# One loop over the edge tiles, with a running maximum, where three loops stood

## The reference

```python
# third layer, last part: agg holds summed edge messages of each node
os1 = ssp(s_in @ w_f2o1_s / sqrt(2F));  os2 = os1 @ w_f2o2_s / sqrt(B)
ov2 = (v_in x w_f2o1_v / sqrt(2F)) x w_f2o2_v / sqrt(B)      # 3 components
x3  = layernorm(x2 + concat([os2, ov2]))

# fourth layer: attention over the edges that leave a node, 8 heads of 64
q, k, v = split(x3 @ W);  q = q * 64 ** -0.5
aw    = einsum('ehf,ehf->eh', q[src], k[dest])
m     = segment_max(aw, src)
e     = exp(aw - m[src])
denom = segment_sum(e, src)
out   = segment_sum(e / denom[src] * v[dest], src)
x4    = layernorm(x3 + out)
```

## Time and profile before

| | us |
|---|---|
| median of the runs shown (3 runs, 2404.39 to 2411.34) | 2409.9 |
| the profiled execution, its time | 2407.1 |
| its span, first to last instruction | 2405.4 |
| PE busy in the span | 1907.2 |
| DVE busy in the span | 1583.2 |
| ACT busy in the span | 1038.4 |
| POOL busy in the span | 1007.9 |

### The profile page before, as it was taken

The page is one execution under the profiler, slowest core; times in us unless marked ns, Lnnn a source line. Parts: engine busy times, 40 slices in busy tenths (PEclk is TensorE's granted clock), DMA queues, the critical chain, the costliest instruction groups (busy, mean ns, idle before and its releaser), DMA issues. The chain is left out here.

```text
span 2405.4 us, 24073 instructions
## 1 busy us (share of the span) xinstructions
PE 1907.2 (79%) x5516; PEld 938.7 (39%) x5516; DVE 1583.2 (66%) x2672; ACT 1038.4 (43%) x1968; POOL 1007.9 (42%) x1095
## 2 busy tenths in 40 slices
PE   5999995999999999999999790055487699967800
PEld 2444442444444444444444340033255444423300
DVE  5464552577777777777776060799568679867854
ACT  2353442455555555555554230244278623313332
POOL 2211112466665666666656532456322012224334
PEclk9999998999999999999999895555568799979855
DMA  7632113444444444444443633433333222227743
GB/s 259 244 130 58 18 22 56 164 158 151 153 158 144 159 155 146 163 147 156 157 142 136 199 64 48 114 84 88 101 126 123 104 90 106 106 79 193 211 136 110
DMA packets 159454, 310.19 MB, mean 129 GB/s; under 512 B 31890, under 2 KB 45107, under 8 KB 159127
## 3 DMA queue, kind: packets, MB, share of 16 engines
q1 hardware_dynamic: 126278, 233.65, 28.0%
q0 software_dynamic: 29760, 71.21, 13.1%
q10 hardware_dynamic: 3344, 4.51, 0.6%
HBM read 169.54 MB, written 139.76 MB: 129 GB/s over the span
## 5 line engine op out<-in xcount | busy, mean ns | idle before, releaser
L659 PE MATMUL d_p_h<-w3a,d_xT 128*128 128x512 f32 x640 | 290.5, 597 | 25.4 <-DMA d_xT<-in_xT 25.4
L659 PE MATMUL d_p_o<-d_w,d_uT 128*128 128x512 f32 x640 | 289.9, 596 | 3.0 <-ACT d_uT L734 3.0
L659 PE MATMUL d_p_p<-d_wr,d_x1T 128*128 128x512 f32 x640 | 289.0, 595 | 0.0
L550 POOL TENSOR_SCALAR d_small<-d_mv 128x1 f32<-128x1 f32 x160 | 81.9, 512 | 303.5 <-DVE d_mv L785 153.7
L816 DVE TENSOR_TENSOR d_zz<-d_yg,d_xbeta 128x512 f32<-128x512 f32 x80 | 138.5, 1731 | 98.9 <-POOL d_yg L867 98.9
L659 PEld LDWEIGHTS d_p_h<-w3a,d_xT 128*128 128x128 f32 x640 | 122.8, 192 | 180.4 <-issue 180.4
L659 PEld LDWEIGHTS d_p_o<-d_w,d_uT 128*128 128x128 f32 x640 | 122.1, 191 | 156.6 <-issue 152.0
L727 ACT ACTIVATE d_yn<-d_y,d_small 128x512 f32<-128x512 f32 x80 | 65.1, 813 | 230.6 <-POOL d_small L555 230.6
L659 PEld LDWEIGHTS d_p_p<-d_wr,d_x1T 128*128 128x128 f32 x640 | 116.1, 191 | 115.9 <-issue 115.9
L282 PE MATMUL m_p_H<-m_xT,m_w 128*128 128x512 f32 x320 | 147.3, 615 | 4.8 <-ACT m_xT L323 4.8
L755 ACT ACTIVATE d_x<-d_zz,d_small 128x512 f32<-128x512 f32 x80 | 65.1, 814 | 178.4 <-POOL d_small L555 178.4
(11 more groups left out here) (252 smaller groups left out, 4239.2 us busy)
## 6 DMA issues: line engine op xcount, KB each, us to landing
sum<-d_zeros SPq DMA_DIRECT2D x80, 260.0 KB, 2.1
sum<-m_tile_sum SPq DMA_DIRECT2D x10, 2048.0 KB, 7.8
d_xT<-in_xT SPq DMA_DIRECT2D x80, 256.0 KB, 2.7
d_z<-sum SPq DMA_DIRECT2D x80, 256.0 KB, 2.9
d_x<-in_x SPq DMA_DIRECT2D x80, 256.0 KB, 3.4
x<-d_x SPq DMA_DIRECT2D x80, 256.0 KB, 2.0
p<-d_p SPq DMA_DIRECT2D x80, 256.0 KB, 2.0
pair_p<-p SPq DMA_DIRECT2D x40, 512.0 KB, 3.8
```

The source lines that it names most:

```text
L550: nc.gpsimd.tensor_scalar(tmp, var, factor, add, ALU.mult, ALU.add).then_inc(done, 1)
L659: last = nc.tensor.matmul(out[:, :], lhsT[:, c, :], w[:, c, :], start=(c == 0), stop=(c == KB - 1))
```

## The change

The three loops become one (`values_phase`, names `f_`), of 25 steps. In step i tile `a = i` has its message sums gathered and its first product, `b = i-1` its second product and x3 rows, `c = i-2` its queries and keys, `d = i-3` its scores, maximum, weights and values, `e = i-4` is merged into the state. The state of a node is one row in a table of 528 floats: 8 heads of 64 sums and one denominator, and 8 maxima. A tile gathers its nodes' rows, takes the larger of the old maximum and its own, weighs its values with reference to that new maximum, scales the old sums by exp(old - new), adds its own sums and writes the rows back; the next tile's gather waits for that write. The two tables of sums and maxima, the gather of final maxima and the accumulating scatter go.

Further parts: the scores are spread by a store to a DRAM row and a load broadcast to 128 partitions, on SP, in place of the diagonal and the product with ones; x2 is added on PE through the identity, the vector part of the second product is written to PSUM with a step of 3, its factor is put into the weights once, and ACT copies the result to `y`; the softplus is done per tile; `p_O`, `p_R`, `p_k` and the tile for queries and values are single; two reciprocals stand in `o_` for one; two table fills per node tile stand for three. The pairs follow a written plan: 3, 2, 2, then 1, 2, 1, 2, ... per step.

```diff
+def plain_plan(steps):
+    plan = [3, 2, 2] + [1 + i % 2 for i in range(steps - 3)]
-                sp.dma_start(rows(k.sum3, i), zeros[:, :]).then_inc(tables_set, 16)
-                sp.dma_start(rows(k.max3, i), lowest[:, :]).then_inc(tables_set, 16)
+                sp.dma_start(rows(k.state, i), empty[:, :]).then_inc(tables_set, 16)
...
         @block.sync
+            for step in range(STEPS):
+                t = step - 3
+                if 0 <= t < T:
+                    sp.wait_ge(aw_done, t + 1)
+                    sp.dma_start(k.aw_rows[t, :].rearrange("(p h) -> p h", h=HEADS), k.scores[:, t, :]
+                                 ).then_inc(aw_out, 16)
+                    sp.wait_ge(aw_out, 16 * (t + 1))
+                    if t:
+                        sp.wait_ge(cand_done, t)
+                    sp.dma_start(spread[:, :, :].rearrange("p e h -> p (e h)"),
+                                 k.aw_rows[t:t + 1, :].to_broadcast([P, P * HEADS])).then_inc(spread_in, 16)
+                for _ in range(HERE[step - 1] if step else 0):
+                    if pair + 2 < PAIRS:
+                        pair_load(nc, k, sp, pair + 2)
+                    pair_store(nc, k, sp, pair)
+                    pair += 1
...
         @block.gpsimd
+            def gather_sums(u):
+                if u >= AHEAD:
+                    n = turn_number((u - AHEAD) // 2, 2 + u % 2)
+                    pool.wait_ge(turned, n + 1)
...
+            def gather_state(t):
+                if t:
+                    pool.wait_ge(gone, 16 * t)
...
+            def scatter_state(t):
+                pool.wait_ge(merged, t + 1)
...
+            for step in range(STEPS):
+                for u in (2 * step + AHEAD, 2 * step + AHEAD + 1):
+                    if u < 2 * T:
+                        gather_sums(u)
+                t = step - 4
+                if 0 <= t < T:
+                    scatter_state(t)
+                    if t + 1 < T:
+                        gather_state(t + 1)
...
         @block.tensor
+            def second(t, s):
...
+                if u:
+                    pe.wait_ge(y_done, u)
...
+                nc.tensor.matmul(p_R[:, :], k.ident[:, :], rows_of(t, s), start=True, stop=False)
+                vector = p_R[:, B:D].rearrange("p (d c) -> p c d", c=3)
+                for c in range(4):
+                    last = nc.tensor.matmul(p_R[:, 0:B] if c == 0 else vector[:, c - 1, :],
+                                            outT[t % 2][:, s, c * P:(c + 1) * P],
+                                            (w2s if c == 0 else w2v)[:, :], start=False, stop=(c == 3))
...
+            for step in range(STEPS):
+                second(b, 0); turn_x3(c, 0); turn_x3(c, 1); second(b, 1); turn_sums(a, 0)
+                queries(c); first(a, 0); turn_sums(a, 1); values(d); first(a, 1); keys(c); tile_sums(d)
...
         @block.scalar
+            for step in range(STEPS):
+                second_product_out(b, 0); x3_turned_out(c, 0); x3_turned_out(c, 1)
+                second_product_out(b, 1); sums_turned_out(a, 0); away_from(d); query_out(c)
+                first_product_out(a, 0); sums_turned_out(a, 1); x3_rows(b); first_product_out(a, 1)
+                weights(d); state_factors(d); logarithms(a)
+                for _ in range(HERE[step]):
+                    pair_normalise(nc, k, act, pair)
+                    pair += 1
...
         @block.vector
+            def new_maximum(t):
+                buf, top = old[t % 2], new[:, ATT:STATE]
+                dve.wait_ge(old_in, 16 * (t + 1))
...
+                nc.vector.tensor_tensor(top, buf[:, ATT:STATE], buf[:, STATE:STATE + HEADS], ALU.max
+                                        ).then_inc(new_top, 1)
...
+                nc.vector.tensor_tensor(less[:, :], k.scores[:, t, :], top, ALU.subtract).then_inc(less_done, 1)
+                nc.vector.tensor_tensor(fall[:, :], buf[:, ATT:STATE], top, ALU.subtract).then_inc(fall_done, 1)
...
+            for step in range(STEPS):
+                scores(d); merge(e); moments(b, 0); moments(b, 1); pair_leaky(pair)
+                if extra == 1: pair_moments(pair)
+                tile_maximum(d)
+                if extra > 1: pair_moments(pair)
+                new_maximum(d); weigh_values(d); scale_state(d); softplus(a)
+                for _ in range(extra - 1): pair_leaky(pair); pair_moments(pair)
```

More of the change, by code:

```diff
@@ L52 @@
 PAIRS = NODE_TILES // 2
-PAIRS_Q, PAIRS_S, PAIRS_V = 10, 14, 16
+STATE = ATT + HEADS
 LOG2 = 0.6931471805599453
@@ L1107, in reciprocal_deviation @@
     act.wait_ge(done, base + 2 + n)
-def spread_over(steps, n):
-    return [(i * n) // steps != ((i + 1) * n) // steps for i in range(steps)]
+def plain_plan(steps):
+    plan = [3, 2, 2] + [1 + i % 2 for i in range(steps - 3)]
+    assert sum(plan) == PAIRS
+    return plan
 def pair_load(nc, k, sp, j):
@@ new lines, in values_phase @@
+        cand = k.filters[:, :, :, :].rearrange("p t c f -> p (t c f)")[:, KB * 2 * D:KB * 2 * D + HEADS * P].rearrange(
+            "p (h e) -> p h e", h=HEADS)
+        away = sb("away", [P, P])
+        less, both = sb("less", [P, HEADS]), sb("both", [P, HEADS, HD + 1])
+        old = [sb(f"old{i}", [P, STATE + HEADS]) for i in range(2)]
+        new = sb("new", [P, STATE])
+        fall, factor = sb("fall", [P, HEADS]), sb("factor", [P, HEADS])
+        p_T = [ps(f"p_T{i}", [P, D]) for i in range(2)]
@@ L1424, in _ @@
         def _(pe):
-            pe.wait_ge(w_in, 64)
[L1427 to L1462, removed]
+            def turn_sums(t, s):
+                u, n = 2 * t + s, turn_number(t, 2 + s)
+                pe.wait_ge(sums_in[u % AHEAD], 16 * (u // AHEAD + 1))
+                if n >= 2:
+                    pe.wait_ge(turned_out, n - 1)
+                for c in range(4):
+                    last = nc.tensor.transpose(p_T[n % 2][0:2 * F, c * P:(c + 1) * P],
+                                               sums[u % AHEAD][:, c * 2 * F:(c + 1) * 2 * F], k.ident[:, :])
+                last.then_inc(turned, 1)
@@ new lines, in product, with queries @@
+            def product(out, xT, w, done):
+                for c in range(KB):
+                    last = nc.tensor.matmul(out[:, :], xT[:, c, :], w[:, c, :], start=(c == 0), stop=(c == KB - 1))
+                last.then_inc(done, 1)
+            def queries(t):
+                pe.wait_ge(turned_out, turn_number(t + 2, 0) + 1)
+                if t:
+                    pe.wait_ge(vw_done, t - 1)
+                    pe.wait_ge(q_out, t)
+                product(p_qv, srcT, k.wqk[:, :, 0:D], q_done)
@@ L1824, in _ @@
+                if 0 <= d < T:
+                    tile_maximum(d)
+                if extra > 1:
+                    pair_moments(nc, k, dve, pair)
+                    pair += 1
+                if 0 <= d < T:
+                    new_maximum(d)
+                    weigh_values(d)
+                    scale_state(d)
+                if a < T:
+                    softplus(a)
+                for _ in range(extra - 1):
                     pair_leaky(nc, k, dve, pair)
@@ L1897, in _ @@
                 b, c = g % 2, g % BUFS
+                heads = [sums[c][:, s, 0:ATT].rearrange("p (h f) -> p h f", h=HEADS) for s in range(2)]
                 dve.wait_ge(sums_in[c], 32 * (g // BUFS + 1))
```

643 lines of the change are left out of this document (290 added, 353 removed).

## The result

The changed kernel takes 2452.99 us (median of 4 runs, 2449.69 to 2454.42) where the kernel before took 2407.14 us on the same chip (4 runs, 2402.78 to 2411.34). The ratio is 1.0191, with a 95% interval of 1.0170 to 1.0213. The forecast was 2454 us. The profiled execution took 2452.36 us against 2407.08 us, so 45.3 us more where +44 had been worked out.

A forecast was written before the change was run, and what follows sets the result against it. A chain across engines, not any engine's work, was taken as the bound. Summed steps ended the rows at 2352 against 2304.0, 48 us more, less up to 5: +44, giving 2451, plus 2.8 for the median: 2454 us, range 2385 to 2510.

The forecast's parts named there:

- The chain of a long step: From softplus to softplus after two pairs, through ACT, PE, POOL and the state's landing and gather: 29.2 us before clock and landings.
- The second path: Beside the chain in long steps: scores' store, broadcast, pair's load at 15.7 us, then pair, maximum and subtractions ending at 25.4.
- POOL's wait: POOL's gather for turned sums stands ahead of the state's scatter, to 18.9 us; removing it wins little in long steps.
- The long step: A step after two pairs: 29 to 37 us, taken as 32; the clock up to 4, landings 3.4 more at worst.
- The start: DVE's first pair at 1733.9 us as before, step 0's softplus at 1742, step 1 29 us; fewer table fills and starts save up to 5.
- The gap from the last rows to the o stage: The 9 us from the last rows' end at 2304.0 to the o stage's start at 2313 were to stay.
- The drain: Five last steps, set by DVE's list: together 87 us, plus 2.6 for the last normalisation, ending at 2352.
- DVE's work: DVE's busy work in the merged loop: 9.0 us a tile and 6.66 a pair, 446 us, 11 below before.
- The costs put at nothing: The maximum's read with step 8, at most double 1.22 us, hidden; the second product's write with step 3, up to 17 us.
- (a): Rival: the work sets the pace, 17 full steps average 23.5 us, 2389 us; gain below 24.7 us a step; chance 0.20.
- (b): Rival: idle stretches keep PE at 1.2 GHz, long steps 38 and short 30 us, 2550 us; chance 0.06.
- (c): Rival: the added chains cancel exactly what two drains give back, 2410 us; chance 0.04.

The follow-up runs named there:

- the six products: Changed kernel with six unread products on PE where it waits for ACT's copy in the long steps: 2452.89 us, ratio 1.0216 to the kernel before.
- The first experiment: Changed kernel with POOL's list alone reordered, the state's scatter and gather ahead of the two gathers of message sums: 2408.41 us, ratio 1.0020.
- POOL's and ACT's order mended: Changed kernel with state ahead of gathers on POOL and the second pair's normalisation moved to the next step on ACT: 2412.71 us, ratio 1.0032.
- the lists mended: Changed kernel with POOL's state first, ACT's second normalisation later and SP's pair loads ahead of the scores' store and broadcast: 2374.13 us, ratio 0.9865.
- ACT's 7 alone: Changed kernel with ACT's list alone changed, a step's second pair normalised in the next step ahead of the x3 rows: 2443.26 us, ratio 1.0160.
- SP's a loss of 12 alone: Changed kernel with SP's list alone changed, pair loads issued ahead of the scores' store and broadcast: 2460.19 us, ratio 1.0239.
- PE doing ten products for nobody: Changed kernel with POOL's and ACT's lists reordered, plus ten unread products before the tile sums of long steps: 2401.52 us, ratio 0.9982.

## Why the prediction held

**The chain of a long step was right link by link.** Counted from the end of the softplus at 2072.12: PE's wait for ACT ends at 9.9 us (forecast 9.9). POOL's gather is issued at 19.4 (17.5 and up to 4 for the clock; 17.7 with the clock kept by the six products), and the scatter at 21.1 (18.9 and the same). The state's row is there at 28.2 (25.8 with nothing for the clock, so up to 29.8 with it), and the softplus ends at 30.9. The second path has its pair's load at 16.2 (15.7) and its maximum and subtractions done at about 26 (25.4). POOL's wait, ACT's turn and DVE's wait for `f_old` stand in the list of waits as named, and PE's granted clock is 0.82 (near 0.8).

**POOL's order was the cause of the loss.** The first experiment moves only it, and 1.0191 becomes 1.0020. "Taking POOL's wait away would thus win little in these steps" is right too: 1.7 us a long step. The gain is in the short steps, 4.8 us each.

**The sum, term by term.** The middle column is the forecast.

| | forecast | measured |
|---|---|---|
| softplus of step 0 ends | 1742 | 1744.5 |
| steps 1 to 3 | 82.5 | 86.2 |
| steps 4 to 16: seven short | 168 | 166.0 |
| six long | 192 | 184.2 |
| steps 17 to 19 | 76.5 | 76.7 |
| draining and last normalisation | 89.6 | 96.1 |
| the end of the rows (2352 in the forecast, rounded up on the way) | 2350.6 | 2353.8 |

The end is right within 3 us, but in part by luck, since errors cancel. Three terms were mis-sized, and one gap.

*The long step* was put 1.3 us too high, 32 for 30.7. The 4 us for the clock and the 3.4 us for landings were given as bounds, and about 2.8 us of them were added to the 29.2. The six unread products show that the clock's part, 1.6 us on the way to the scatter, has no effect on the end of these steps. The forecast took the pair's traffic as mostly over by the landing, and that is so only because the scatter is late. Where the clock does cost, 1.4 us in a short step behind a pause, it does so only with POOL's and ACT's order mended.

*The start.* The end of table fills was to give back up to 5 us; the first gather of the loop is at 1730.7 where the kernel before had it at 1727.7. These 3 us arise ahead of the loop: the last scatter of the loop before it is issued at 1720.3 for 1717.3. One profile can't price such a term, since the first softplus starts anywhere from 1736.0 to 1747.6 in the twelve profiled executions of the changed kernel and its variants. Step 1 took 32.0 us for 29. These are the rows of the loop's start and end, which answer to the earlier trace rows and to the o stage's start in the earlier trace rows:

```profile
1730.74 1.02 POOL L1482 DMA_INDIRECT f_sums<-sum,index  x1 [8.86 <-POOLq L541]
...
2331.49 1.71 POOL L1493 DMA_INDIRECT state<-f_new,unique  x1 [14.41 <-DVE f_new L1809]
...
2352.26 1.52 ACT L1171 ACTIVATE pair_rows<-pair_rows,pair_shift,pair_rstd 128x512 f32<-128x512 f32 x2
...
2358.27 0.97 POOL L1870 DMA_INDIRECT o_sums<-state,index  x1 [25.07 <-PEq L1851]
```

The gap from the last rows to the o stage is 4.5 us, where 9 had been kept. That is why the span comes to +45.2 us with the last rows 50 later than in the earlier trace rows. The timeline of POOL in the kernel before shows what filled the 9 us:

```profile
2302.64 1.55 POOL L1773 DMA_INDIRECT sum<-v_tile_sum,unique  x1 [4.00 <-DMA sum<-v_tile_sum,unique]
2313.04 1.02 POOL L1873 DMA_INDIRECT o_sums<-sum,index  x1 [8.85 <-PEq L1854]
```

There the last accumulating scatter is issued together with the last rows, and the phase ends only behind its landing (6.3 us in the median). In the changed kernel the last scatter is issued 22 us before the last rows end, so that nothing of it is left to wait for. By these two traces, which no further run backs, the forecast kept a wait that the change had taken away.

*The drain* took 96.1 us for 89.6. DVE's timeline shows where:

```profile
2292.38 1.22 DVE L1138 TENSOR_TENSOR pair_p<-pair_p,bn_scale 128x1024 f32<-128x1024 f32 x1 [7.83 <-DMA pair_p<-p]
...
2311.85 2.00 DVE L1768 TENSOR_TENSOR filters<-same_dst,f_away 128x1024 f32<-128x1024 f32 x1 [1.46 <-DMA same_dst<-aw_rows]
...
2321.95 0.17 DVE L1789 TENSOR_TENSOR f_new<-f_old 128x8 f32<-128x8 f32 x1 [3.98 <-DMA f_old<-state,index]
```

The wait of 7.83 us for the pair's load and that of 1.46 us for the broadcast are the ones forecast. Not forecast is the 3.98 us in step 22 for the state's row: the forecast took DVE's list as the bound there, while the scatter, landing and gather were still in front. And the strided maximum takes 0.8 us more than the sum had for it in each of steps 20, 21 and 22. In the first two nothing hides it; in step 22 it stands ahead of that wait, which would be longer without it.

*DVE's work.* 446 us were forecast and 446.9 measured, but that is luck too. The prediction's removed and added terms, 62 and 28 us, make 34 less than before and not the 11 that its list gives, and the list leaves out the 16 us that the strided maximum added.

**The costs put at nothing.** The strided write of the second product costs nothing: 354 ns a pass against 352, and the same time of the kernel. The Trainium skill (PSUM — Partial Sum Buffer, Specifications (TRN2), the row on cachelines) states that a non-contiguous access pattern slows matmuls significantly; these runs don't bear it out for float32 products of 128 columns with a step of 3. The strided read of the maximum costs 0.78 us, under the double that was allowed for. It was called hidden by DVE's spare time, and for the steady steps of the changed kernel the trace speaks for that, since DVE waits behind the maximum for the state's row, 14 times and 40.3 us in the stage. With the lists mended it is worth 11 to 15 us.

**The rivals.** (a), the work sets the pace, does not hold for the kernel as changed: its full steps average 26.8 us and not 23.5. But its break-even of 24.7 us was a fair measure. POOL's list alone gives 24.3 us a step, for which the rule says 7 us less than before, and 5 more were measured; all three lists give 23.05, for which it says 17 x 1.65 = 28 us less, and 32 were measured. The work of one loop is smaller than that of three, as (a) had it; the orders of the queues kept it from showing. (b), a low clock throughout, is out with a granted clock of 0.82 and short steps of 23.7 us. The Trainium skill (TensorE: Matmul & The Clock Gate, Part 1) has a loop with DMA waits swing between two levels; the doubled tile sums behind a pause agree, 2.10 us at a granted clock of 0.50 against 1.14 us at 1.00; PE waited there for DVE, and DVE for a load. (c) is out by the interval.

## What to carry to other kernels

When several loops are made one, each engine's list joins waits that had nothing to do with each other, so look on each queue, those of DMA issues included, for the step of the longest recurrence that stands behind a wait of another kind, and put the recurrence first. Price the second and third path before moving anything: here POOL's list was worth 41 us alone, ACT's 7 alone and nothing on top of it, SP's a loss of 12 alone, and the three 79 us together. See what bulk transfers stand ahead of a small one on which the recurrence waits: the same scatter was followed by its gather after 3.0 us or after 5.6, by how close the pair's loads were. A cost that is hidden now must be costed again after each such move, since the one that hid under a wait (a strided read, 11 to 15 us) becomes the bound when the wait goes.

## What was not expected of the hardware

A pass of DVE over 1024 float32 columns read with a step of 8 elements took 2.00 us against 1.22 us read in order. Float32 matmuls writing PSUM with a step of 3 elements took the same time as plain ones. The scatter of the state took a median of 2.8 us to land in the changed kernel, 4.9 us with SP's loads next to it, and 6.0 us with POOL's list moved, where it is issued just ahead of the broadcast and the pair's loads (2052.20 and 2052.75); the short steps of the last did not suffer by it. PE doing ten products for nobody, 8.75 us of work, made a kernel faster by 12 us through the clock of what followed.
